# Token ranks, places and flags made group by group inside the sequence loop, in a decoder layer with routed experts

## The reference

```
logits = xf @ Wr.T + br
expert_idx = jnp.argmax(logits, axis=-1)
h = jax.nn.relu(jnp.einsum('td,efd->etf', xf, W1) + b1[:, None, :])
y = jnp.einsum('etf,edf->etd', h, W2) + b2[:, None, :]
out = y[expert_idx, jnp.arange(xf.shape[0])]
```

## Time and profile before

| | |
|---|---|
| median of 3 runs | 370.98 us (370.13 to 372.14) |
| the profiled execution | 371.73 us, its span 369.8 us, 6464 instructions |
| TensorE busy | 325.6 us, 88% of the span |
| VectorE busy | 211.4 us, 57% |
| GpSimd busy | 201.5 us, 54% |
| ScalarE busy | 151.8 us, 41% |
| mean granted TensorE clock | 0.95 |

### The profile page before, as it was taken

The page is one execution under the profiler, slowest core; times in us unless marked ns, Lnnn a source line. Parts: engine busy times, 40 slices in busy tenths (PEclk is TensorE's granted clock), DMA queues, the critical chain, the costliest instruction groups (busy, mean ns, idle before and its releaser), DMA issues.

```text
span 369.8 us, 6464 instructions
## 1 busy us (share of the span) xinstructions
PE 325.6 (88%) x1892; PEld 258.7 (70%) x1893; DVE 211.4 (57%) x439; ACT 151.8 (41%) x383; POOL 201.5 (54%) x321
## 2 busy tenths in 40 slices
PE   1999879999899999999987128999999999999980
PEld 1455436557677787778775127899999999999960
DVE  4999993525977687778742472244344434434431
ACT  2788845247443453354353100523422432342220
POOL 5789960325678658776762133055455554655652
PEclk9999989999999999999998655999999999999996
DMA  7900000512556656653640564001101100011110
GB/s 209 352 8 1 3 0 0 181 28 51 167 152 202 186 152 177 170 182 99 210 140 27 211 270 156 2 28 43 31 32 29 37 31 29 28 35 38 28 44 21
DMA packets 17030, 35.04 MB, mean 95 GB/s; under 512 B 3456, under 2 KB 8327, under 8 KB 16360
## 3 DMA queue, kind: packets, MB, share of 16 engines
q1 hardware_dynamic: 14840, 30.01, 25.7%
q0 software_dynamic: 1872, 4.59, 4.2%
q10 hardware_dynamic: 288, 0.07, 0.1%
HBM read 30.99 MB, written 4.20 MB: 95 GB/s over the span
## 4 chain that ended last, share of the span: by engine, by line
PE 76%; DVE 11%; POOL 3%; ACT 3%; DMA 3%; issue 2%; SPq 0%; DVEq 0%; POOLq 0%; ACTq 0%
PE ps L1417 18%; PE ps L1435 17%; DVE stage_b L957 7%; PE ps L1347 7%; PE ps L1327 7%; PE ps L1225 6%; PE ps L1272 4%; PE ps L1368 4%; PE ps L1273 3%; PE ps L1372 2%; DMA w<-in_x_t 2%; PE ps L1200 1%; PE ps L1404 1%; PE ps L1379 1%; DMA stage_b<-x_rows,stage_b 1%
## 5 line engine op out<-in xcount | busy, mean ns | idle before, releaser
L1417 PEld LDWEIGHTS ps<-stage_b 128*128 128x128 f32 x576 | 69.9, 199 | 2.6 <-DVE stage_b L1149 1.0
L1417 PE MATMUL ps<-stage_b 128*128 128x128 f32 x576 | 70.3, 282 | 1.2 <-ACT stage_b L900 1.2
L1435 PE MATMUL ps<-w,stage_b 128*128 x288 | 65.2, 380 | 1.1 <-DVE stage_b L1174 1.1
L1435 PEld LDWEIGHTS ps<-w,stage_b 128*128 128x128 f32 x288 | 53.3, 190 | 8.0 <-issue 1.5
L1008 DVE TENSOR_TENSOR stage_b<-ps,w 112x512 f32<-112x512 f32 x64 | 39.7, 683 | 23.5 <-PE ps L1273 21.4
L632 POOL TENSOR_TENSOR stage_b<-stage_b 112x512 f32<-112x512 f32 x16 | 21.4, 1339 | 44.5 <-DVE stage_b L1008 32.3
L900 ACT ACTIVATE stage_b<-ps 128x256 f32<-128x256 f32 x19 | 7.3, 385 | 85.0 <-PE ps L1404 85.0
L891 ACT ACTIVATE stage_b<-ps,b 128x128 f32<-128x128 f32 x144 | 39.2, 383 | 7.2 <-issue 7.2
L673 POOL DMA_INDIRECT stage_b<-x_rows,stage_b x21 | 31.4, 1496 | 9.7 <-issue 5.5
L1149 DVE COPY stage_b<-w 128x2048 f32 x19 | 24.2, 1275 | 21.3 <-issue 14.3
L1327 PEld LDWEIGHTS ps<-consts,stage_b 112*128 112x128 f32 x256 | 31.0, 192 | 7.1 <-issue 6.6
(11 more groups left out here) (164 smaller groups left out, 528.5 us busy)
## 6 DMA issues: line engine op xcount, KB each, us to landing
w<-in_w SPq DMA_DIRECT2D x16, 512.0 KB, 4.2
w<-in_w SPq DMA_DIRECT2D x16, 256.0 KB, 3.0
w<-in_w SPq DMA_DIRECT2D x4, 1024.0 KB, 8.8
stage_b<-in_ctx SPq DMA_DIRECT2D x16, 224.0 KB, 2.8
w<-in_x_t SPq DMA_DIRECT2D x4, 448.0 KB, 6.8
stage_b<-in_x SPq DMA_DIRECT2D x16, 112.0 KB, 3.0
x_rows<-stage_b SPq DMA_DIRECT2D x16, 112.0 KB, 1.9
w<-in_w_in SPq DMA_DIRECT2D x2, 512.0 KB, 5.6
```

What stands on the lines that cost most here:

```text
L1417: last_ = m.matmul(ps[:, 2 * par + f // 4, (f % 4) * P:(f % 4 + 1) * P], w1_now[par][:, k, f * P:(f + 1) * P], rows_t[:, par, k * P:(k + 1 ...
L1435: last_ = m.matmul(ps[:, 4 + par, 0:D], h_t[:, par, f * P:(f + 1) * P], w2[:, e, f, :], start=(f == 0), stop=(f == FT - 1))
```

## The change

The 16 sequences are cut into five groups of 4, 4, 2, 4 and 2. For groups 0 to 3 the work moves into the sequence loop:
- `rank_token(g)` (VectorE) makes the group's flags: at the end of steps 8 and 12, behind the four products of step 14, and at the start of step 18.
- `count_group(g)` (GpSimd) adds up flags over sequences into `counted`, at the start of steps 9, 13, 15 and 19.
- `rank_group(g)` (TensorE) makes ranks over all earlier sequences directly: a triangle product, a product of ones with `counted`, and one for each earlier sequence of the group; in steps 9, 13, 14 and 18, between the output projection and the transposes of s - 4.
- `find_slot(g)` (VectorE) splits the rank into a tile and a place and makes `in_place`, at the end of steps 9, 13, 14 and 18.

Group 4 is done behind the loop, with one sum of all flags for the experts' totals. The tile number is then the rank's tile plus the first tile of the token's expert. `in_place` now lies in the room of W2's expert 6, which is therefore loaded last, once the token products are done. The two number parts go through one product per sequence with 42 columns, and VectorE adds the two halves. Buffers of the expert stage move to other places.

The diff, cut to what runs on the engines; of the old routing the removed lines are left out (they stand in the kernel above):

```diff
+GROUPS = ((0, 4), (4, 4), (8, 2), (10, 4), (14, 2))
...
+        place_at = (NE // 2 + 2) * FT * D
+        in_place = w2_flat[0:L, place_at:place_at + NB * P // 2].bitcast(BF16).rearrange("p (b n) -> p b n", b=NB)
...
+        q = Region(stage_b[:, 2 * DT * FF:r.used], r.used - 2 * DT * FF)
+        one_hot = q.cut(NB * NE // 2, L).bitcast(BF16)
+        counted = q.cut(len(GROUPS) * NE // 2, L).bitcast(BF16).rearrange("p (g e) -> p g e", e=NE)
+        key, ranked = q.cut(CB * NE, L), q.cut(CB * NE, L)
+        best, first = q.cut(CB, L), q.cut(CB, L)
+        tile_in, part_in = q.cut(NB, L), q.cut(NB, L)
+        ones8 = q.cut(NE)
...
         def count_bank(n):
             return 5 - n // 2 % 2
+        def rank_of(g):
+            return ps[0:L, 2, 64 * (g % 2):64 * (g % 2) + GROUPS[g][1] * NE]
+        total_ps = ps[:, 2, 128:128 + NE]
+        token_at = ps[:, 2, 256:256 + 2 * TILES]
         def z_bank(unit):
...
             sp.dma_start(shared[:, :], ins["b2"].to_broadcast([P, NE * D])).then_inc(loaded["b2"], 16)
-            for e in range(NE // 2, NE):
-                if e == NE - 1:
-                    sp.wait_ge(rows_loaded[0], 16)
+            for e in (4, 5, 7, 6):
+                if e == 6:
+                    sp.wait_ge(token_ps, 1)
                 sp.dma_start(w2[:, e, :, :], ins["w2"][:, e, :, :]).then_inc(loaded["w2"], 16)
...
+                if 2 * pair + q in (9, 13, 15, 19):
+                    count_group((9, 13, 15, 19).index(2 * pair + q))
...
+            def count_group(g):
+                nonlocal counted_at
+                b0, n = GROUPS[g]
+                pool.wait_ge(one_hot_set, g + 1)
+                for b in range(b0, b0 + n):
+                    need(pool, counted_step, counted_at)
+                    last = g_.tensor_tensor(counted[:, g + 1, :], counted[:, g + (b > b0), :],
+                                            one_hot[:, b * NE:(b + 1) * NE], ALU.add)
+                    last.then_inc(counted_step, 1)
+                    counted_at += 1
...
+            ranked_at = 0
+            def then_next(ins_):
+                nonlocal ranked_at
+                ranked_at += 1
+                ins_.then_inc(rank_step, 1)
+                dve.wait_ge(rank_step, ranked_at)
+            def rank_token(g):
+                b0, n = GROUPS[g]
+                be = lambda x: x.rearrange("p (b e) -> p b e", e=NE)
+                lg, k_, m8 = be(logits[:, b0 * NE:(b0 + n) * NE]), be(key[:, 0:n * NE]), be(const("expert_m8", L)[:, 0:n * NE])
+                dve.wait_ge(logit_set, b0 + n)
+                if g == 0:
+                    then_next(v.memset(ones8, 1.0))
+                    then_next(v.memset(counted[:, 0, :], 0.0))
+                then_next(v.tensor_reduce(best[:, 0:n], lg, AX_X, ALU.max))
+                then_next(v.tensor_tensor(k_, lg, best[:, 0:n].unsqueeze(2).to_broadcast([L, n, NE]), ALU.is_equal))
+                then_next(v.tensor_tensor(k_, k_, m8, ALU.mult))
+                then_next(v.tensor_reduce(first[:, 0:n], k_, AX_X, ALU.min))
+                v.tensor_tensor(be(one_hot[:, b0 * NE:(b0 + n) * NE]), m8,
+                                first[:, 0:n].unsqueeze(2).to_broadcast([L, n, NE]), ALU.is_equal).then_inc(one_hot_set, 1)
+            def find_slot(g):
+                b0, n = GROUPS[g]
+                be = lambda x: x.rearrange("p (b e) -> p b e", e=NE)
+                t_, p_ = tile_in[:, b0:b0 + n], part_in[:, b0:b0 + n]
+                dve.wait_ge(rank_ps, g + 1)
+                then_next(v.tensor_tensor(ranked[:, 0:n * NE], rank_of(g), one_hot[:, b0 * NE:(b0 + n) * NE], ALU.mult))
+                then_next(v.tensor_reduce(p_, be(ranked[:, 0:n * NE]), AX_X, ALU.add))
+                then_next(v.tensor_scalar(t_, p_, 1 / P, 0.5 / P - 0.5, ALU.mult, ALU.add))
+                then_next(v.tensor_scalar(t_, t_, MAGIC, MAGIC, ALU.add, ALU.subtract))
+                then_next(v.scalar_tensor_tensor(p_, t_, -float(P), p_, ALU.mult, ALU.add))
+                for b in range(b0, b0 + n):
+                    v.tensor_scalar(in_place[:, b, :], iota16[:, :], part_in[:, b:b + 1], None, ALU.is_equal)\
+                     .then_inc(place_set, 1)
+            dve.wait_ge(tri_set, 2)
             def step(pair, q):
+                if 2 * pair + q == 18:
+                    rank_token(3)
                 b, par, half = seq(pair, q, 0)
                 if b is not None:
...
+                if 2 * pair + q == 14:
+                    rank_token(2)
                 if (pair, q) == (0, 0):
...
+                if 2 * pair + q in (8, 12):
+                    rank_token((2 * pair + q - 8) // 4)
+                if 2 * pair + q in (9, 13):
+                    find_slot((2 * pair + q - 9) // 4)
+                if 2 * pair + q in (14, 18):
+                    find_slot((2 * pair + q - 6) // 4)
                 if (pair, q) == (1, 0):
                     dve.wait_ge(fall_step, 2)
...
+            rank_token(len(GROUPS) - 1)
+            find_slot(len(GROUPS) - 1)
             dve.wait_ge(x2t_set, NB)
             for q in range(2):
                 dve.wait_ge(x2_stored[q], 16 * NB // 2)
...
+            tiles_of, run_, from_ = per_e[:, 0, :], per_e[:, 1, :], per_e[:, 2, :]
+            link(v.tensor_scalar(tiles_of, total_ps, 1 / P, (P - 1) / P + 0.5 / P - 0.5, ALU.mult, ALU.add))
+            link(v.tensor_scalar(tiles_of, tiles_of, MAGIC, MAGIC, ALU.add, ALU.subtract))
+            link(v.tensor_tensor_scan(run_, ones8, tiles_of, 0.0, ALU.mult, ALU.add))
+            link(v.tensor_tensor(from_, run_, tiles_of, ALU.subtract))
+            be = lambda x: x.rearrange("p (b e) -> p b e", e=NE)
+            link(v.tensor_tensor(be(from_tile), be(one_hot), from_[0:L].unsqueeze(1).to_broadcast([L, NB, NE]), ALU.mult))
+            link(v.tensor_reduce(slot_tile, be(from_tile), AX_X, ALU.add))
+            link(v.tensor_tensor(slot_tile, slot_tile, tile_in, ALU.add))
             v.tensor_tensor(in_tile, slot_tile.unsqueeze(2).to_broadcast([L, NB, TILES]),
                             const("iota", L)[:, 0:TILES].unsqueeze(1).to_broadcast([L, NB, TILES]), ALU.is_equal)\
              .then_inc(in_tile_set, 1)
...
             dve.wait_ge(token_ps, 1)
...
+            link(v.tensor_reduce(token_f, token_at.rearrange("p (s i) -> p i s", s=2), AX_X, ALU.add))
+            v.tensor_scalar(token_of, token_f, float(T), None, ALU.add).then_inc(token_set, 1)
             link(v.tensor_tensor(tile_hits.rearrange("p (i e) -> p i e", e=NE),
...
+            def rank_group(g):
+                b0, n = GROUPS[g]
+                pe.wait_ge(ones_set, 1)
+                pe.wait_ge(tri_set, 2)
+                pe.wait_ge(one_hot_set, g + 1)
+                need(pe, counted_step, b0)
+                hot = lambda b: one_hot[:, b * NE:(b + 1) * NE]
+                o = rank_of(g).rearrange("p (b e) -> p b e", e=NE)
+                m.matmul(rank_of(g), tri16[:, :], one_hot[:, b0 * NE:(b0 + n) * NE], start=True, stop=False)
+                last_ = m.matmul(o, ones16[0:L, 0:L], counted[:, g, :].unsqueeze(1).to_broadcast([L, n, NE]),
+                                 start=False, stop=False)
+                for i in range(n - 1):
+                    last_ = m.matmul(o[:, i + 1:n, :], ones16[0:L, 0:L],
+                                     hot(b0 + i).unsqueeze(1).to_broadcast([L, n - 1 - i, NE]),
+                                     start=False, stop=(i == n - 2))
+                if g < len(GROUPS) - 1:
+                    last_.then_inc(rank_ps, 1)
             def step(pair, q):
                 if (pair, q) != (0, 0):
...
+                if 2 * pair + q in (9, 13):
+                    rank_group((2 * pair + q - 9) // 4)
+                if 2 * pair + q in (14, 18):
+                    rank_group((2 * pair + q - 6) // 4)
...
-            pe.wait_ge(ones_set, 1)
-            pe.wait_ge(one_hot_set, 1)
-            pe.wait_ge(tri_set, 2)
-            m.matmul(ps[0:L, 0, 0:NB * NE], tri16[:, :], one_hot, start=True, stop=True)
-            m.matmul(ps[:, 1, 0:NB * NE], ones16[0:L, :], one_hot, start=True, stop=True).then_inc(rank_ps, 1)
+            rank_group(len(GROUPS) - 1)
+            b0, n = GROUPS[-1]
+            m.matmul(total_ps, ones16[0:L, :], counted[:, len(GROUPS) - 1, :], start=True, stop=False)
+            for b in range(b0, b0 + n):
+                last = m.matmul(total_ps, ones16[0:L, :], one_hot[:, b * NE:(b + 1) * NE], start=False,
+                                stop=(b == NB - 1))
+            last.then_inc(rank_ps, 1)
             pe.wait_ge(parts_set, 2)
             for b in range(NB):
                 pe.wait_ge(place_set, b + 1)
-                for part in range(2):
-                    last = m.matmul(ps[:, 2, 0:TILES], in_place[:, b, :], token_parts[:, b, part, :],
-                                    start=(b == 0 and part == 0), stop=(b == NB - 1 and part == 1))
```

(26 more changed lines are left out.)

54 lines of the change are left out of this document (8 added, 46 removed).

## The result

The changed kernel is slower: 375.28 us median (374.38 to 378.49, 4 runs) against 371.48 (370.13 to 372.14, 4 runs), ratio 1.0108 with a 95% interval of 1.0074 to 1.0141. The forecast was 372.0 with a range of 368.4 to 374.8, so the time lies outside it. The profiled execution took 374.87 us with a span of 373.1, 3.3 more than before.

A forecast was written before the change was run, and what follows sets the result against it. TensorE was taken to bound the sequence loop, latencies its end, and VectorE's routing the stretch behind it. Loop +2.6, routing -2.4, gather +0.8 gave +1.0 us: span 370.8, 372.7 for that execution, 372.0 as median; range 368.4 to 374.8.

The forecast's parts named there:

- what it had named to look at: Signs in the changed profile: line 1008, last logits, routing stretch, gather landing, TensorE idle in step 14, VectorE idle in step 15.
- the loop: Sequence loop to the last logits: 2.6 us longer, 0.3 of it for VectorE and GpSimd meeting; bounds 0.6 and 4.0.
- the gather: First gather behind the token list: lands 0.8 us later beside expert 6's weight transfer; ends 0 and 2.3.
- the routing: Last logits' addition to token list: 2.4 us saved, 8.7 instead of 11.12; bounds 1.7 and 3.0.
- 9.9 us without a pause, to 182.2: VectorE in steps 13 to 15: unbroken work, so the last sequence's four products start 2.3 us late.
- locked out by GpSimd: Rival for steps 13 to 15: VectorE's moved flags wait for GpSimd, +1.3 us, 373.3; chance 0.12.
- the other half of that rule: In the loop: a VectorE tensor_scalar in faster modes and a GpSimd instruction exclude each other for a whole instruction.
- TensorE also waits for the flags of group 2, from 176.9 to 177.5, but VectorE is later still: Step 14: TensorE's wait for flags sets no pace, VectorE does; TensorE idle under 1 us.
- The clock: Rival: 1.6 us regained in the first tile or lost at the loop's end; chance 0.06, a third fast.
- The token products: Routing behind the loop: 16 products of 42 columns at 0.08 to 0.10 us each, 1.5 us.
- the gather comes fully behind expert 6's weights: Rival at the first gather: 2.3 us late instead of 0.8, 373.5; chance 0.20.
- the transfer's rest is short by then: Argument against the gather rival: little of the weight transfer, forecast to end at 223.4, remains when the gather is issued.

The follow-up runs named there:

- e1: Changed kernel with one input of each flag operation (key, best, first) in PSUM instead of SBUF; 372.73 us, ratio 1.0028.
- e11: Kernel before plus three chained VectorE operations in step 14 (a reduction, two multiplications of 112x16 with SBUF inputs), results unused; 372.35 us in one run.
- e2: Changed kernel with group 2's flags at the end of step 13 instead of behind step 14's four products; 371.37 us in one run.
- e4: Kernel before with one token product of 42 columns for each sequence and the extra reduction; 372.41 us in one run.
- e9: Changed kernel with group 2's flags at the end of step 13 and W2 of experts 7 and 6 behind the first gather; 369.99 us, ratio 0.9934.
- e6: Changed kernel with groups 1 and 2's work moved out of steps 13 to 15, expert 6 alone still behind the token products; 371.94 us, ratio 0.9999.
- e7: Changed kernel with groups 1 and 2's work moved out of steps 13 to 15, W2 of experts 7 and 6 behind the first gather; 368.54 us, ratio 0.9920.
- e5: Kernel before without the hold on W2 of the last expert, 7, until the first gather has landed; 371.70 us, ratio 1.0000.
- e13: Kernel before with W2 of experts 6 and 7 both held behind the first gather; 371.78 us, ratio 1.0013.
- e10: Kernel before plus two independent VectorE multiplications of 112x16 in step 14, both inputs in SBUF, results unused; ratio 0.9982.
- e3: Changed kernel with W2 of experts 7 and 6 both held until the first gather has landed; 373.86 us, ratio 1.0052.

## Why the prediction was wrong

Of what it had named to look at, two things came: VectorE has no idle time ahead of step 15's products, and the gather lands more than 4 us after issue. Line 1008's last group of four (5.5 us late, not 2.3), the last logits' addition (213.18, not 210.5), the stretch to the token list (7.59, not 8.7) and TensorE's idle time in step 14 (2.74, not under 1) came otherwise. Against their forecasts the loop (1.6 us), the gather (1.9) and the head (1.0) came out worse, the routing (1.1) and the first tile (1.5) better. The head and the first tile are no part of the change's mechanism as far as is known, and it is luck that they nearly cancel.

**The loop on VectorE: the failed step.** "9.9 us without a pause, to 182.2" priced group 2's flags at 1.0 us. They took 3.1, since lines 1046 and 1047 each waited out a GpSimd operation (e1, e11). The prediction looked for such meetings among the place flags and the other tensor_scalars alone; its rival "locked out by GpSimd" had the right engine, but its +1.3 was priced from the place flags' 0.53 each; the comparison (1046) and the multiplication (1047) that did wait cost 1.1 and 1.0 us each, and with TensorE's clock 3.6 together. The place flags took 0.25 each in the loop, at most 0.255, none of them blocked. The load by itself was over-sized: 2.3 forecast, 1.5 measured (e2).

The Trainium skill ("SBUF — State Buffer", Who interferes with whom) says that a VectorE instruction with two SBUF inputs contends with a GpSimd instruction that reads SBUF. The trace agrees: 1.26 and 1.19 us beside GpSimd, 0.17 behind the loop, 0.18 with one input in PSUM. The prediction had weighed only the other half of that rule, on the faster modes.

**The loop on TensorE.** "TensorE also waits for the flags of group 2, from 176.9 to 177.5, but VectorE is later still" was wrong twice: the wait was 2.74 us, and behind it VectorE was not the later engine but waited 1.80 us for TensorE's line 1441, which stood at half clock. No term stood for what followed on TensorE, 3.5 us mostly at 1.2 GHz, worth about 1.5. The clock stood in the prediction as a rival of 1.6 us either way, placed at the loop's end and not in the middle of it. The 1.9 of e1, 2.1 (idle) and 1.5 (clock) make the 5.5 us at the last line 1079. Only 4.2 of them reach the last logits, because the kernel before had its own slow stretch in between, 1.15 us by e4. Such stretches come and go with the execution: e2 and e9 have the same loop and the same last line 1079 (72.92 and 72.91), yet the last logits' addition is 99.39 behind the mark in e2 and 100.87 in e9, whose clock is at half from 202.9 to 206.3.

**The routing.** Flags, rank wait, slots and tiles came within 0.2 us of their forecasts. The token products were the mis-sized term, 1.5 against 0.74: I took their 81 ns for the engine's own pace, and it was VectorE's (e4). The prediction also read that GpSimd's token numbers opened the products; in the trace it is the first place flag (to 216.13, the numbers to 216.08), which changes the sum by nothing to speak of. The saving is 3.53, above the upper bound of 3.0.

**The first gather.** Forecast +0.8, at most 2.3; measured +2.65. The mechanism was the rival's, "the gather comes fully behind expert 6's weights", which was set aside since "the transfer's rest is short by then". It is not: a token list that comes 7.6 us behind the logits, instead of the 8.7 forecast, finds 5 MB still moving, whose traffic lasts about 13 us from the loop's end, and the wait grows as the routing shrinks. Saving and price were one term, not two.

**The first tile.** It took 5.26 instead of 6.72 us: the clock rose sooner. The forecast had nothing here. In e1, e2, e6 and e7 the same 32 products took 6.63, 5.44, 6.54 and 6.72, and with the old routing 6.72 (before), 5.47 (e5) and 5.14 (e13), so it follows neither the change nor the gather's wait. What decides it stays open, and so does why e9's twelve runs fall into two groups (four at 366.5 to 367.3, the others at 369.0 to 370.9) and where the last 0.4 us of the changed kernel comes from.

## What to carry to other kernels

Before moving small VectorE operations into a full loop, list those with two SBUF inputs and look at what GpSimd does at that moment; each can cost a whole GpSimd operation, here 1.26 us, and a chain of them meets the next one too. Put one input in PSUM, or place them in GpSimd's gap. When a stretch is shortened that ends in a transfer, first find what is queued ahead of the transfer: e6 saved 3.5 us in the routing and gave nearly all of it back (its rows come 0.3 earlier), and one wait moved (e7) kept it.

## What was unexpected of the hardware

- An instruction that waits for GpSimd shows as a long one (1.26 us for 112x16), not as idle time, so the sum of an engine's busy time hides it.
- Whether two instructions meet is a matter of 0.1 us: in e10 two of them began 0.1 to 0.2 us ahead of GpSimd's and did not wait (GpSimd's took 1.51 instead of 1.34), in e11 one began 10 ns behind it and took 1.29.
- A gap of 2.74 us in a full loop was followed by 3.5 us mostly at 1.2 GHz, in both profiles of the changed kernel and in e3; one of 0.68 (e1) was not.
- At 1.2 GHz, bf16 products of 42 columns with a new 112x128 weight each start 36 ns apart (16 of them, 0.54 us from the first start to the last).
- The gather, on GpSimd's queue, was not served beside 400 GB/s of weights on SyncE's: issued some 5 us before their end, it moved its first packet 4.2 us later instead of 1.9, when they thinned out, and delivered behind them (e6: 387 GB/s in 220 to 222, 129 in 222 to 224, rows at 223.83).
